# Two-layer graph attention on one core: self edges moved from the dense stage and the end of a node update to the start of the same layer's node update

## The reference, cut to what matters

```python
src = jnp.concatenate([edge_index[0], loops])
dst = jnp.concatenate([edge_index[1], loops])
for l in range(L):                      # 2 layers
    ...                                 # layer norm, degree and position terms
    q, k, v = ...                       # (n, 8 heads, 16)
    att = jnp.einsum('ehd,ehd->eh', q[dst], k[src]) / scale
    att = nan_to_num(clip(att, -50, 50))
    ex = exp(att - m[dst]);  s = segment_sum(ex, dst)
    aggr = segment_sum(v[src] * (ex / s[dst]), dst)
    x = x + (aggr @ Wo[l] + bo[l])
    h = gelu(layernorm(x) @ W1[l] + b1[l]);  x = x + (h @ W2[l] + b2[l])
```

## Time and profile before

| what | value |
|---|---|
| median of 3 runs | 3553.08 us (3547.33 to 3558.46) |
| profiled execution, first to last instruction | span 2632.1 us, 60679 instructions |
| outside that span (median less span) | 921 us |
| busy in the span | PE 80%, PEld 67%, DVE 75%, ACT 67%, POOL 69% |
| mean granted TensorE clock | 0.931 of full speed |
| chain that ended last | POOL 46%, issue 21%, PE 17%, DVE 9%, DMA 3% |

### The profile page before, as it was taken

The page is one execution under the profiler, slowest core; times in us unless marked ns, Lnnn a source line. Parts: engine busy times, 40 slices in busy tenths (PEclk is TensorE's granted clock), DMA queues, the critical chain, the costliest instruction groups (busy, mean ns, idle before and its releaser), DMA issues.

```text
span 2632.1 us, 60679 instructions
## 1 busy us (share of the span) xinstructions
PE 2104.4 (80%) x13853; PEld 1757.0 (67%) x13854; DVE 1978.7 (75%) x7060; ACT 1766.3 (67%) x4889; POOL 1805.2 (69%) x1967
## 2 busy tenths in 40 slices
PE   6989978766788888888888876677788778778877
PEld 6988943355677677676677755566666666666766
DVE  6898958756788888888888865677777777776775
ACT  6766756465677677677677735567677777777763
POOL 5746445477777777777777726777777777777773
PEclk9999989789999999999998887999999999999998
DMA  7867723233344434434444413333343333333332
GB/s 213 263 210 223 223 81 122 94 104 106 114 117 121 123 115 121 122 116 122 120 116 121 121 56 102 106 110 114 110 115 114 109 114 113 109 114 113 110 113 62
DMA packets 187155, 327.00 MB, mean 124 GB/s; under 512 B 38950, under 2 KB 100963, under 8 KB 186864
## 3 DMA queue, kind: packets, MB, share of 16 engines
q0 software_dynamic: 80208, 216.22, 28.6%
q1 hardware_dynamic: 105632, 106.77, 13.1%
q10 hardware_dynamic: 1024, 1.06, 0.1%
HBM read 291.56 MB, written 20.71 MB: 119 GB/s over the span
## 4 chain that ended last, share of the span: by engine, by line
POOL 46%; issue 21%; PE 17%; DVE 9%; DMA 3%; ACT 2%; DVEq 2%; POOLq 1%; ACTq 0%; SPq 0%
POOL arena L2131 44%; PE bank L1121 7%; DMA arena<-kv_rows,idx_stage 3%; PE bank L2222 2%; PE bank L1126 1%; DVE aggregate L2270 1%; PE bank L1856 1%; DVE arena L2278 1%; PE bank L2213 1%; PE bank L1850 1%; POOL norm_stat L1402 1%; DVE bn L1569 1%; DVEq L2259 1%; ACT arena L1507 1%; PE bank L1446 1%
## 5 line engine op out<-in xcount | busy, mean ns | idle before, releaser
L2131 POOL DMA_INDIRECT arena<-kv_rows,idx_stage x1612 | 1525.4, 946 | 552.0 <-issue 489.3
L2222 PE MATMUL bank<-arena 128*128 128x136 f32 x3328 | 602.5, 315 | 231.7 <-DVE aggregate L2270 225.4
L2222 PEld LDWEIGHTS bank<-arena 128*128 128x128 f32 x3328 | 486.4, 206 | 336.6 <-DVE aggregate L2270 241.3
L2213 PE MATMUL bank<-queries,arena 128*128 x3328 | 496.1, 296 | 182.0 <-DVE arena L2291 143.5
L2213 PEld LDWEIGHTS bank<-queries,arena 128*128 128x128 f32 x3328 | 439.7, 205 | 237.6 <-issue 235.3
L2270 DVE TENSOR_TENSOR aggregate<-bank,aggregate 128x136 f32 x1664 | 492.9, 296 | 122.5 <-PE bank L2222 49.6
L2291 DVE TENSOR_TENSOR arena<-bank,arena 128x512 f32<-128x512 f32 x416 | 286.8, 690 | 363.5 <-DMA arena<-kv_rows,idx_stage 294.9
L2152 ACT ACTIVATE arena<-iota_n,at_negdst 128x128 f32<-128x128 f32 x1664 | 527.8, 395 | 2.9 <-DMA queries<-arena 1.8
L2163 ACT ACTIVATE arena<-bank 128x512 f32<-128x512 f32 x416 | 247.2, 594 | 209.7 <-PE bank L2198 192.0
L2278 DVE TENSOR_TENSOR arena<-arena,bank 128x512 f32<-128x512 f32 x416 | 282.4, 679 | 20.3 <-ACT arena L2179 20.3
L2198 PE MATMUL bank<-ident,arena 128*128 128x128 f32 x1664 | 271.2, 289 | 19.0 <-ACT arena L2157 19.0
(11 more groups left out here) (336 smaller groups left out, 2768.8 us busy)
## 6 DMA issues: line engine op xcount, KB each, us to landing
arena<-in_edge_attr_dram SPq DMA_DIRECT2D x244, 256.0 KB, 3.5
arena<-kv_rows,idx_stage POOLq DMA_INDIRECT x1612
kv_rows<-arena SPq DMA_DIRECT2D x12, 512.0 KB, 3.8
kv_rows<-arena SPq DMA_DIRECT2D x24, 256.0 KB, 2.1
queries<-in_x_dram SPq DMA_DIRECT2D x13, 256.0 KB, 3.8
arena<-in_x_dram SPq DMA_DIRECT2D x12, 256.0 KB, 4.0
x_rows<-arena SPq DMA_DIRECT2D x12, 256.0 KB, 2.9
x_stream<-arena SPq DMA_DIRECT2D x12, 256.0 KB, 2.3
```

The source lines that it names most:

```text
L2131: pool.indirect_dma_start(kv[:, n, :], None, kv_dram[l], bass.IndirectOffsetOnAxis(idx_stage[:, half % 2, n:n + 1], 0)).then_inc(Z.kv_in[s ...
L2213: m = pe.matmul(bank[:, ATT_BANK[1][r % 2], j * D:(j + 1) * D], sel_t[:, r % SELT_SLOTS, j, :], q_all[:, bass.ds(tiles[j], 1), :].rearrang ...
L2222: pe.matmul(sums_of(j), sel[:, r % SEL_SLOTS, j, :], msg[:, r % 2, j, :], start=True, stop=True).then_inc(Z.sum, 1)
```

## The change: what it does

In the dense stage VectorE's self edges and ScalarE's exponential are gone. ScalarE clears `aggregate` of the unit (128 numbers per node) behind `h1`. In a node update, each unit (in both layers) first loads its own K|V rows back from DRAM (`own`, 256 KB for two tiles, started by SyncE in slot 0), computes product, sum, clip and mask product in gaps 3 to 6 of round 0, the exponential on ScalarE in slot 0, v times weight in gap 3 of round 1 into a scratch (`ownm`), and adds this to the sums in gap 6 of round 1 (`total`). `guard` adds the weight along with its constant. In layer 0, `aggregate` is cleared in gap 3 of round 2 in place of writing the next self edges, and slots 14 and 15 keep only q, k, v and the stores. For the last two units of a layer the self edges are computed ahead, in rounds 4 and 5 of the layer's first body.

```diff
-                "act": ("z0", "zt_sb", "h1_sb", "h2_sb", "z1", "z2", "z3", "xt_sb", "exp"),
-                "dve": ("o",) + norm_steps(1) + norm_steps(2) + norm_steps(3) + each("qkv", t) + SELF,
+                "act": ("z0", "zt_sb", "h1_sb", "clear", "h2_sb", "z1", "z2", "z3", "xt_sb"),
+                "dve": ("o",) + norm_steps(1) + norm_steps(2) + norm_steps(3) + each("qkv", t),
...
                 if a:
                     act.wait_ge(*done("pe", "h1", a))
                     move(a, 0, h1_t[a.b], ACT.Relu, bias=cols_0[:, 0:1])
+                    act.activation(a.nodes(agg), ones_f[:, 0:1].unsqueeze(1).to_broadcast([P, a.t, D]), ACT.Copy, scale=0.0
+                                   ).then_inc(unit_sem("act", a), 1)
...
                 if e:
                     project(e, (2, 3))
-                    loop_logits(e)
-                    if not a and not final_unit(e):
-                        held.append(e)
-                    else:
-                        loop_messages(e)
...
+        AHEAD_SLOTS = (4, 5)
...
-               "qkv0": (14, 0), "qkv1": (14, 1), "prod": (14, 2), "logit": (14, 3), "clip": (14, 4), "att": (14, 5),
-               "weights": (15, 0), "self": (15, 1)}
+        GAP = {"prod": (0, 3), "logit": (0, 4), "clip": (0, 5), "att": (0, 6), "message": (1, 3), "total": (1, 6),
...
         def sp_update(sp, l):
             def stages(r, u):
+                if r == SLOT["own"] and u.own:
+                    if u.again:
+                        sp.wait_ge(*u_before(u).done("dve", "message"))
+                        sp.sem_inc(Z.turn, 1)
+                    sp.dma_start(u["own"], u.rows(kv_dram[l])).then_inc(update_move["own", u.b], 16)
...
+                if r == SLOT["exp"] and u.own:
+                    act.wait_ge(*u.done("dve", "att"))
+                    act.activation(u.atts(5), u.atts(2), ACT.Exp).then_inc(own_exp[u.b], 1)
...
+                if at == GAP["message"]:
+                    dve.wait_ge(*u.weighed())
+                    count(u, dve.tensor_tensor(heads(u["ownm"]), heads(u["own"][:, :, D:2 * D]), per_head(u.atts(5), u), ALU.mult), 0)
...
+                if at == GAP["total"]:
+                    dve.wait_ge(*u.done("dve", "message"))
+                    if u.again:
+                        dve.wait_ge(*u_before(u).done("pe", "up0"))
+                        dve.sem_inc(Z.turn, 1)
+                    count(u, dve.tensor_tensor(u["z"], u.nodes(agg), u["ownm"], ALU.add), 0)
                 if at == GAP["guard"]:
-                    count(u, dve.tensor_scalar(u.atts(3).rearrange("p (t h) -> p t h", h=HEADS), u.nodes(agg, D, MW), SUM_GUARD, None, ALU.add), 0)
+                    count(u, dve.scalar_tensor_tensor(out=u.atts(3).rearrange("p (t h) -> p t h", h=HEADS), in0=u.nodes(agg, D, MW),
+                                                      scalar=SUM_GUARD, in1=u.atts(5).rearrange("p (t h) -> p t h", h=HEADS),
+                                                      op0=ALU.add, op1=ALU.add), 0)
...
+                    if at == GAP["clear"]:
+                        dve.tensor_scalar(u.nodes(agg, 0, MW), ones_f[:, 0:1].unsqueeze(1).to_broadcast([P, u.t, MW]), 0.0, None, ALU.mult)
```

More of the change, by code:

```diff
@@ L1268, in each @@
             return tuple(f"{name}{k}" for k in range(n))
-        SELF = ("prod", "logit", "number", "clip", "att", "self")
+        OWN = ("prod", "logit", "number", "clip", "att", "message", "total")
         def steps_of(who, t):
@@ L1463, in free @@
                 if u.again:
-                    pe.wait_ge(*done("dve", "self", u, 1))
+                    pe.wait_ge(*done("dve", f"qkv{UNIT - 1}", u, 1))
             def mlp_step(a, c, d, e):
@@ L1521, in free @@
                             act.wait_ge(*moved(name, u, 1))
-            held = []
             def mlp_step(a, c, d, e):
@@ L1531, in mlp_step @@
                     move(e, 1, t_sb[e.b])
-                while held:
-                    exp(held.pop())
                 if a and not first_unit(a):
@@ L1626, in mlp_step @@
                     project(e, (0, 1))
-                while held:
-                    loop_messages(held.pop())
                 if d:
@@ L1682, in gnn_kernel, with __init__ @@
         update_move = {(name, b): sem(f"update_{name}{b}") for name in UPDATE_TRANSFERS for b in SETS}
+        own_exp = sems("own_exp", len(SETS))
         class Updated:
-            def __init__(self, l, j, base, b=0):
+            def __init__(self, l, j, base, b=0, ahead=False):
                 self.l, self.j, self.base, self.b = l, j, base, b
+                self.own, self.nodes_too = ahead or b == 0, not ahead
                 self.t = UPDATE_TILES[b]
@@ L1772, in __call__ @@
                 begins, ends = counted or newest >= 0, counted or newest > 0
+                if not counted and i == 0 and h == 0 and r in AHEAD_SLOTS:
+                    base = self.load(FULL - 1, 1)[0]
+                    for u in (Updated(self.l, 0, base, 1, True), Updated(self.l, 0, NT - 1, 2, True)):
+                        self.stages(AHEAD_SLOTS.index(r), u, *gap)
                 if r == 0 and gap in ((), (self.loads_at,)):
@@ L1869, in stages @@
             def stages(r, u, gap):
+                if not u.nodes_too:
+                    return
                 if r == SLOT["up"]:
```

94 lines of the change are left out of this document (35 added, 59 removed).

## The result

The kernel after takes 3577.78 us (median of 6 runs), the kernel before beside it 3550.20: ratio 1.0081, 95% interval 1.0056 to 1.0106, 0.8% slower. 3545 us was forecast. To read this one must know that the first profiled execution of before (span 2632.1 us) ran its attention stages at another pace than the timed runs that the forecast was made against. Profiled again, the kernel before shows a span of 3549.3 us at a time of 3551.03. So only 1.7 us lie outside the span, and nearly all of the 921 us that the prediction put there are time of the two attention stages.

A forecast was written before the change was run, and what follows sets the result against it. GpSimd's gathers were taken to bound attention, a chain not through the self edges the dense step. Savings 4.7 + 0.5 + 1.4 + 0.6 = 7.2 us, with 0.8 more 8 us, gave 3545 us; 8-in-10 range 3528 to 3562.

The forecast's parts named there:

- the 921 us: Time of the timed runs beyond the profiled span of 2632.1 us, said to hold nothing that is changed.
- The bound: Both attention stages run at GpSimd's pace: gathers 1.25 us each, 1,007 us per layer if nothing makes GpSimd wait.
- slack of 20 us: Attention stages: VectorE may fall some 20 us further behind before the 8-round ring makes GpSimd stand still.
- The new wait: Layer 0 units: message waits for an exponential behind four GELUs and two table loads; at worst some 3 us, valued 0.
- Rival 2: Layer 0: the new wait makes VectorE late beyond what the ring absorbs, no gain, 3548 to 3560 us; chance 0.18.
- Dense stage: VectorE's self edges are not on the step's chain; 4.7 us saved over ten steps, 0.5 us at the stage's end.
- GpSimd's multiply: Dense stage, L1404: falls from 0.67 to 0.20 us without VectorE's product beside it, 0.47 us a step.
- rival 1: VectorE does set the dense step: 3.2 us less in ten steps, 32 us, 3519 us with the tails; chance 0.12.
- The clear on ScalarE: Dense stage: valued at nothing, from above 0.65 us in 13 steps, 8.5 us.
- Layer 1's steady part: New VectorE work of 2.4 us per unit, 57 us in all, hidden by gather waits; value 0, from above +57.
- Tails and hand-over: Ends of the layers: 1.4 us off layer 0's last rounds, 0.6 us off its last stores.
- Rival 3: Attention stages: new VectorE instructions block the gathers, +30 us on the bound, 3575 us; chance 0.10.

The follow-up runs named there:

- e0: The kernel before, unchanged, profiled once more: 3551.03 us, span 3549.3 us.
- e9: The kernel before plus a ScalarE exponential of constants behind the older unit's GELUs, VectorE waiting for it at the message's place: ratio 1.0065.
- e5: The kernel before plus a VectorE wait for the older unit's last GELU at the message's place, no computing instruction added: ratio 1.0014.
- e1: The kernel after with the self edges' exponential issued ahead of the older unit's four GELUs: 3535.72 us, ratio 0.9965.
- e15: The kernel after, unchanged, timed again where before takes about 2640 us: 2629.05 us, ratio 0.9973.
- e17: The kernel before, unchanged, profiled again at the pace of about 2640 us: span 2630.6 us.
- e16: The kernel after with the exponential ahead of the GELUs and message and total later, at the pace of about 2640 us: 2618.56 us, ratio 0.9943.
- e2: The kernel after with all self edges left out (loads, product, sum, exponential, message, total), clears kept: 3528.67 us, ratio 0.9938.
- e6: The kernel after with the exponential ahead of the GELUs in layer 0 only: ratio 0.9974.
- e4: The kernel after with the message moved from gap 3 to 7 and total from 6 to 8, exponential still behind the GELUs: ratio 0.9966.

## Why the prediction was wrong, step by step

**The bound**: right for the execution that was profiled, and read as that of the timed runs. The step that failed is the sentence "The 921 us outside the span hold nothing that is changed": by e0 they are 455 us in layer 0's gathers, 415 in layer 1's, 41 behind the two, 6 ahead of the first gather, and 4 left over between span and median. At that pace GpSimd waits 915 us for VectorE, so the ring has no slack of 20 us left, and a delay of VectorE ahead of an add can cost: 3.4 us a unit did (e9), 2.3 us did not visibly (e5).

**The new wait**: the prediction saw it, and what is queued behind it (the adds, and TensorE behind them). Its length, "at worst some 3 us per unit", was right at the 2640 pace (2.5 us in the mean of 44, 3.3 the longest) and too short at the other (3.8 us in the mean of 36, 5.8 the longest). It valued it at 0, since "both fit in the 20 us". That is the term that failed: it costs the 42 us between after and e1. Rival 2 had the mechanism, but it too let the ring absorb the first 20 us. By e15 a lag that the ring hides is not absorbed where the next stage waits for VectorE. It is paid at the end of the layer: the last add came 14.8 us later behind the last gather, and the hand-over grew by 14.3. That it was "a shift of a wait that is there already one round later" fell too: e9 adds it to before, and it costs 23 us. What makes up the other 19 of the 42 us (after waits 135 us; e9 waits 104 and has no own steps behind the wait) was not separated.

**Dense stage**, -4.7 and -0.5 forecast, -14.2 measured at the 2640 pace. GpSimd's multiply fell as forecast: ten of its 39 cases took 0.66 to 0.74 us in e17, and in e15 all take 0.19 or 0.20 us. In the mean (e17, then e15, columns as in the earlier trace rows):

```profile
L1404 POOL TENSOR_TENSOR norm_stat<-norm_stat 128x4 f32<-128x4 f32 (+1 forms) x39 | 12.6, 323 | 3.1
```

```profile
L1408 POOL TENSOR_TENSOR norm_stat<-norm_stat 128x4 f32<-128x4 f32 (+1 forms) x39 | 7.8, 200 | 3.1
```

That gives about 0.5 us in each of ten steps, 4.8 us together against 4.7 forecast. But the nine steps in the middle of the stage, which took between 12.3 and 13.9 us in e17, take 11.8 or 11.9 in e15. The rest is rival 1 in part. In e17's step the chain runs over the self edges:

```profile
456.53 0.70 DVE arena L1597
...
458.67 1.23 DVE att_self L1605
...
461.07 0.88 DVE bn L1569 x4
```

The statistics behind them start 10.6 us after the row add (450.43). In e15 they start 9.0 us after it (441.31), and wait for GpSimd:

```profile
450.28 0.87 DVE L1561 BATCH_NORM_STATS2 bn<-arena 128x6 f32<-128x128 f32 x4 [2.92 <-POOL arena L1417]
```

The prediction read one step, in which the other path was last. In before the two seem to be near ties, and a chain names only the later; by how much each shortens the step was not measured by itself. The clear on ScalarE cost nothing visible, as valued.

**Layer 1's steady part**, valued at 0 with 57 us from above: right at the 2640 pace (1010.4 against 1008.1 us, of which e16 shows 1007.9), and at the other one small: e2 against e1 prices the own steps of both layers together at 7 to 10 us. The waits that layer 1 adds there are not to be told from no cost (e6 against e1).

**Tails and hand-over**, -2.0 us forecast: -3.6 in e16 (49.2 against 52.8), so nearly of the right size once the lag is gone; in after +14.3 at the 2640 pace (e15) and +2.7 at the other.

**Rival 3**: out as a cost of 30 us. Gathers take 950 and 947 ns in e15 and e16 against 947 in e17, and e16 has all the new instructions. The 3 ns of e15 are 4.7 us over 1612 gathers, which is what its two stretches of gathers are longer (2.4 and 2.3 us).

The range 3528 to 3562 ended 16 us short. At the 2640 pace the forecast of -8 us met -7 us by luck, by two errors that cancel: 9 us more from the dense stage, and the lag.

## What to carry to other kernels

First set the profiled span beside the timed runs: where they differ by more than the 1.7 us that lay outside the span here, the profile may show another execution than the one to be predicted, and the missing time is the first question. A short result that another engine needs is issued ahead of a long block with table loads (e1: 42 us). The instruction that waits for it can also be put later, so that it finds less to wait for and has fewer adds behind it (e4); which of the two helps was not separated. A ring hides a lag from the engine that fills it, but the lag is paid at the next point where all must be done (14.3 us here).

## What the runs showed of the hardware

- The same kernel takes 2635 us (chip 0) or 3550 us (chip 5). The difference lies almost wholly in the attention stages, where TensorE's semaphores were raised 2 to 3 us late on average in the slower case, at either level of the clock. Half the gathers' bytes left this as it was, fewer matmuls nearly so (2.2 and 2.5 us). Late raisings come in bursts, 94 to 95% of them within 1 us behind a landing of a gather, against 57 to 60% of random moments. The cause is open: the runs with half of the gathers and with none met the pace where nothing is late, so none shows what the gathers do to it.
- VectorE's short instructions stretch beside GpSimd as GpSimd's do beside VectorE: L1605 (128x32) took 1.21 us at 458.67 in e17, where GpSimd had begun a 128x512 multiply at 458.57 (it ended at 459.83, L1605 at 459.88), and 0.19 us at 527.35 in e0, beside no instruction of GpSimd. The Trainium skill (page "SBUF — State Buffer", section "SBUF: two separate sides") has this as one port pair held for a whole instruction, and the trace agrees.
- A change of ScalarE's table took 1.28 us each way, and a GELU block between two exponentials made a 0.22 us exponential end 5.1 us behind the round's other two (1289.94 to 1295.02 in after).
